# A selective-scan block with a binary MLP: padded loads of u and B, and another order of VectorE's scan step

## What is computed

```python
xc = silu(conv(normed @ in_proj_W[:, :E]) + conv_b)
dt = clip(softplus(xc @ dt_W + dt_b), 0.001, 0.1)      # (8, 512, E)
Bp, Cp = xc @ B_W, xc @ C_W                            # (8, 512, N)
def step(h, ins):                                      # h: (8, E, N)
    x_t, dt_t, B_t, C_t = ins
    dA = exp(dt_t[..., None] * A)
    h = dA * h + dt_t[..., None] * B_t[:, None, :] * x_t[..., None]
    return h, einsum('ben,bn->be', h, C_t)
_, y = scan(step, h0, (xc, dt, Bp, Cp))                # 512 steps in time
y = y * silu(z);  x = x + y @ out_proj_W;  x = x + ffn(rmsnorm(x))
```

## Time and profile before

| what | value |
|---|---|
| median of 3 runs | 1122.29 us (1107.89 to 1122.53) |
| profiled execution, own time | 1115.98 us |
| its span, first to last instruction | 1114.2 us |
| granted TensorE clock, mean | 0.960 |
| PE busy | 967.9 us (87%) |
| DVE busy | 935.2 us (84%) |
| ACT busy | 908.7 us (82%) |
| POOL busy | 847.9 us (76%) |
| DMA moved | 327.39 MB, mean 294 GB/s |

### The profile page before, as it was taken

One profiled execution on the slowest core, in us unless ns is written; L12 is line 12 of the kernel. 1 busy time (PEld: TensorE's weight loads), 2 busy tenths in 40 slices (PEclk: granted clock), 3 DMA queues, 4 the chain that ended last, 5 costly groups with the idle time before them and its releaser, 6 DMA issues.

```text
span 1114.2 us, 27718 instructions
## 1 busy us (share of the span) xinstructions
PE 967.9 (87%) x8006; PEld 426.6 (38%) x8006; DVE 935.2 (84%) x2131; ACT 908.7 (82%) x1093; POOL 847.9 (76%) x1216
## 2 busy tenths in 40 slices
PE   5998883668999999998999887899998899999897
PEld 3555540113333343433333332334343334343436
DVE  5677663799989999997998887899998899999983
ACT  1666776789999999997988887899997899998980
POOL 6555513789888889887888786898887788988880
PEclk9999996789999999999999999899999899999999
DMA  4234358999999999997999999799999799999940
GB/s 139 81 136 180 136 200 298 345 327 355 351 343 334 345 355 350 345 344 268 356 341 332 319 328 318 271 351 352 353 349 333 280 366 343 339 356 340 335 148 10
DMA packets 76758, 327.39 MB, mean 294 GB/s; under 512 B 13472, under 2 KB 32800, under 8 KB 41504
## 3 DMA queue, kind: packets, MB, share of 16 engines
q1 hardware_dynamic: 76576, 325.30, 83.6%
HBM read 303.24 MB, written 22.02 MB: 292 GB/s over the span
## 4 chain that ended last, share of the span: by engine, by line
DVE 27%; PE 25%; POOL 19%; issue 16%; DMA 5%; ACT 5%; SPq 2%; DVEq 1%; POOLq 0%; ACTq 0%
POOL decayed L593 13%; DVE ps L1221 9%; PE ps L798 8%; DVE state L1232 7%; PE ps L743 5%; PE ps L897 5%; DMA decay<-dt_stage 4%; PE ps L883 3%; DVE h L1336 2%; ACT state L1030 2%; DVE h L1345 1%; DVE soft L1147 1%; POOL soft L543 1%; SPq L392 1%; POOL u_rest L553 1%
## 5 line engine op out<-in xcount | busy, mean ns | idle before, releaser
L593 POOL TENSOR_TENSOR decayed<-decay,state 128x256 f32<-128x256 f32 x1024 | 725.5, 733 | 169.1 <-DVE state L1232 125.4
L1010 ACT ACTIVATE decay<-decay,a_col 128x2048 f32<-128x2048 f32 x256 | 512.7, 2003 | 46.3 <-DMA decay<-dt_stage 36.5
L1232 DVE TENSOR_TENSOR state<-decayed,ps 128x256 f32<-128x256 f32 x1024 | 403.1, 417 | 55.4 <-POOL decayed L593 40.0
L1221 DVE TENSOR_TENSOR ps<-decay,ps 128x512 f32<-128x512 f32 x512 | 352.6, 689 | 40.5 <-ACT state L1030 17.2
L1030 ACT COPY state<-ps 128x512 f32<-128x512 f32 x512 | 288.9, 582 | 64.6 <-issue 43.2
L798 PE MATMUL ps<-state,c_cols 128*32 128x256 f32 x4096 | 338.2, 403 | 0.1
L743 PE MATMUL ps<-moving,b_rows 64*128 64x256 bf16 x1024 | 204.3, 281 | 100.5 <-DVE ps L1221 96.3
L750 PE MATMUL ps<-moving,b_rows 64*128 64x256 bf16 x1024 | 205.4, 282 | 12.0 <-DMA b_rows<-b_stage 12.0
L883 PE MATMUL ps<-h,w 128*128 128x256 f32 x512 | 175.8, 429 | 1.0 <-DVE h L1336 0.8
L743 PEld LDWEIGHTS ps<-moving,b_rows 64*128 64x128 bf16 x1024 | 58.4, 94 | 274.0 <-DVE ps L1221 172.3
L798 PEld LDWEIGHTS ps<-state,c_cols 128*32 128x32 f32 x4096 | 82.0, 109 | 113.4 <-issue 101.3
(11 more groups left out here) (124 smaller groups left out, 825.3 us busy)
## 6 DMA issues: line engine op xcount, KB each, us to landing
decay<-dt_stage SPq DMA_DIRECT2D x512, 512.0 KB, 6.6
moving<-u_stage SPq DMA_DIRECT2D x64, 288.0 KB
b_stage<-b_parts SPq DMA_DIRECT2D x24, 384.0 KB, 3.8
b_rows<-b_stage SPq DMA_DIRECT2D x64, 144.0 KB
dt_stage<-dt_tok SPq DMA_DIRECT2D x8, 512.0 KB, 3.1
u_stage<-u_parts SPq DMA_DIRECT2D x8, 512.0 KB, 2.8
x_tok<-in_L_attn_x_dram SPq DMA_DIRECT2D x4, 512.0 KB, 3.5
u_stage<-u_parts SPq DMA_DIRECT2D x8, 256.0 KB, 2.1
```

The costliest lines, as they stand in the source:

```text
L593: nc.gpsimd.tensor_tensor(decayed[:, p], decay[:, dec_slot(m, k), p, k % TS, :], state[:, (k - 1) % RING, p * E:(p + 1) * E], ALU.mult).th ...
L1010: nc.scalar.activation(pair, pair, ACT.Exp, scale=a_col[:, 2:3]).then_inc(decay_ready, 1)
L1221: nc.vector.tensor_tensor(ps[:, acc_bank(m, k), :].rearrange("p (q e) -> p q e", q=HQ), decay[:, dec_slot(m, k), HQ:Q, k % TS, :], ps[:, a ...
L1232: nc.vector.tensor_tensor(state[:, k % RING, p * E:(p + 1) * E], decayed[:, p], ps[:, SELFP + k % 2, p * E:(p + 1) * E], ALU.add).then_inc ...
```

## The change

Two things. First, u_stage and b_stage get a fourth part, NS = NP + 1, that holds zeros. A load of u now reads 16 rows and writes each four times, to 64 partitions, every second one; a load of B reads and writes 64 rows. So all 128 rows of `moving` are written by loads, and the two memsets of `moving` go; those of `b_rows` stay. The zeros are stored once to DRAM in the prologue, by three DMAs for each batch (`store_pads`), from a part of `moving` that POOL fills with zeros. Second, DVE's step does the first self pair's sum ahead of the product in PSUM and the second behind it, then y's copy. PE's, ACT's and POOL's programs of the scan stay as they are.

```diff
-    ROWS = NP * NP * HALF
-    RSTEP = 3
-    RFIRST = HROW + RSTEP - 1 - RSTEP * (ROWS // 2)
+    NS = NP + 1
+    ROWS = NS * NS * HALF
+    assert HQ * ROWS == P
-    u_stage = nc.dram_tensor("u_stage", (HQ, HQ, 2, NP, T, E), BF16, kind="Internal").ap()
+    u_stage = nc.dram_tensor("u_stage", (HQ, HQ, 2, NS, T, E), BF16, kind="Internal").ap()
-    b_stage = nc.dram_tensor("b_stage", (HQ, HQ, 2, NP, NP, T, 2 * N), BF16, kind="Internal").ap()
+    b_stage = nc.dram_tensor("b_stage", (HQ, HQ, 2, NS, NS, T, 2 * N), BF16, kind="Internal").ap()
         def product_rows(hq):
-            first = RFIRST - 2 + hq
-            return slice(first, first + RSTEP * (ROWS - 1) + 1, RSTEP)
+            return slice(hq, P, HQ)
...
-                         .unsqueeze(1).broadcast_to([HALF * NP, NP, TC * E])
+                         .unsqueeze(1).broadcast_to([HALF * NS, NS, TC * E])
...
+                def store_pads(n):
+                    q, bb = n // 2, n % 2
+                    u_rows, b_planes = u_stage[q % HQ, q // HQ, bb], b_stage[q % HQ, q // HQ, bb]
+                    zeros = moving[:, 1, 0:2 * NS].rearrange("p t e -> p (t e)")
+                    sp.dma_start(u_rows[NP].rearrange("(p j) e -> p (j e)", j=NJ),
+                                 zeros[:, 0:NJ * E]).then_inc(pads_stored, 16)
+                    sp.dma_start(b_planes[NP].rearrange("k (p j) n -> p k (j n)", j=NJ),
+                                 zeros[:, 0:NS * NJ * 2 * N].rearrange("p (k n) -> p k n", k=NS)).then_inc(pads_stored, 16)
+                    sp.dma_start(b_planes[0:NP, NP].rearrange("k (p j) n -> p k (j n)", j=NJ),
+                                 zeros[:, 0:NP * NJ * 2 * N].rearrange("p (k n) -> p k n", k=NP)).then_inc(pads_stored, 16)
...
+                sp.wait_ge(pad_zeroed, 1)
+                for n in range(B):
+                    store_pads(n)
                 for q in range(Q):
...
                 sp.wait_ge(rows_zeroed, 2)
+                sp.wait_ge(pads_stored, 16 * PADS)
...
+                nc.gpsimd.memset(moving[:, 1, 0:2 * NS], 0.0).then_inc(pad_zeroed, 1)
...
-                    nc.gpsimd.memset(moving[:, 0], 0.0)
...
-                    nc.vector.memset(moving[:, 1], 0.0)
...
+                    def add_self(p):
+                        wait_step(dve, self_decayed[p], t)
+                        nc.vector.tensor_tensor(state[:, k % RING, p * E:(p + 1) * E], decayed[:, p],
+                                                ps[:, SELFP + k % 2, p * E:(p + 1) * E], ALU.add
+                                                ).then_inc(self_state[p], 1)
+                    wait_step(dve, self_input, t)
+                    wait_step(dve, contracted, t - RING)
+                    add_self(0)
                     dve.wait_ge(acc_state, t + 1)
                     wait_step(dve, acc_copied, t - NACC)
                     nc.vector.tensor_tensor(ps[:, acc_bank(m, k), :].rearrange("p (q e) -> p q e", q=HQ),
...
                                             ).then_inc(acc_decayed, 1)
+                    add_self(1)
                     chunk = i * 2 + k // TC
                     if k % TC == LAG and not (known(t) and t < TC):
                         keep_y(chunk - 1, i + k // TC - 1, (k // TC + 1) % 2)
-                    wait_step(dve, self_input, t)
-                    wait_step(dve, contracted, t - RING)
-                    for p in range(Q // 2):
-                        wait_step(dve, self_decayed[p], t)
-                        nc.vector.tensor_tensor(state[:, k % RING, p * E:(p + 1) * E], decayed[:, p],
...
```

More of the change, by code:

```diff
@@ L46, in mamba_and_binary_mlp_block @@
     HROW = P // 2
-    ROWS = NP * NP * HALF
-    RSTEP = 3
-    RFIRST = HROW + RSTEP - 1 - RSTEP * (ROWS // 2)
-    assert RFIRST > 0 and HROW + HQ - 1 + RSTEP * (ROWS // 2) <= P
+    NS = NP + 1
+    ROWS = NS * NS * HALF
+    assert HQ * ROWS == P
     QE = Q * E
@@ L118, in mamba_and_binary_mlp_block @@
         b_loaded = [sem("b_loaded0"), sem("b_loaded1")]
+        pad_zeroed = sem("pad_zeroed")
         rows_zeroed = sem("rows_zeroed")
+        pads_stored = sem("pads_stored")
         const_set = sem("const_set")
@@ L212, in mamba_and_binary_mlp_block @@
         STORES = 2 + NP
+        PADS = 3 * B
         def batches(eng, slot, filling=None):
@@ L1227, in step @@
                         keep_y(chunk - 1, i + k // TC - 1, (k // TC + 1) % 2)
-                    wait_step(dve, self_input, t)
-                    wait_step(dve, contracted, t - RING)
-                    for p in range(Q // 2):
-                        wait_step(dve, self_decayed[p], t)
-                        nc.vector.tensor_tensor(state[:, k % RING, p * E:(p + 1) * E], decayed[:, p],
-                                                ps[:, SELFP + k % 2, p * E:(p + 1) * E], ALU.add
-                                                ).then_inc(self_state[p], 1)
                     if known(i) and i == 0:
```

## The result

The changed kernel takes 1406.06 us (median of 4 runs, 1401.68 to 1407.72), the kernel before 1122.41 us beside it (4 runs, 1107.89 to 1129.42). The ratio is 1.2575, with a 95% interval of 1.2452 to 1.2698: slower, as forecast, by 284 us where 239 were forecast. The time lies in the range of 1295 to 1435, 51 us above the forecast of 1355. The profiled execution spans 1403.1 us.

A forecast was written before the change was run, and what follows sets the result against it. DVE's own instructions set a 1.65 us step; the new order makes it 2.16. Scan 1037 + 81 + 10 + 20 = 1148 against 909, +239 on the profiled 1115.98, loads and pads zero: 1355 us, range 1295 to 1435.

The forecast's parts named there:

- The ring: In each scan step, DVE's product, PE's input products, contraction, DVE's first sum, next product: 2.16 us against 1.65.
- y's copy: DVE's copy, now behind the second sum, delays the contraction opening each 16-step chunk: 0.33 us in 31 chunks, 10 us.
- The loads and the pads under cover: Larger scan loads (57 to 62 us per 32 steps of 69) and the prologue's stores of zeros stay hidden: nothing.
- The clock in the first steps: First 32 scan steps, little finishing work on PE, clock partly low: 2.6 us a step, between 2.16 and 2.91.
- The later steps: The other 480 scan steps, with PE 71% busy and at full clock: 2.16 us each, 1037 us.
- the 20 us of waits that were kept: In the scan, 6.5 us for the first loads and 13.6 us of DVE's product behind ACT's exponential stay.
- The front: Before the scan, first loads add 2 us, dropped memsets save; together zero (-2 to +2).
- (a): Rival: TensorE at half clock for much of the scan, 2.91 us a step: 1724 us, half of them about 1540; chance 0.08.
- (b): Rival: in the scan the loads bind at 352 GB/s, not DVE's new order: +39, 1155 us; chance 0.05.
- (c): Rival: faster, as POOL starts its first pair sooner and DVE idles less in the scan: at most 61 us, 1055; chance 0.04.
- (d): Rival: both effects, of order and loads, stay under 1% each: 1105 to 1140 us; chance 0.03.

The follow-up runs named there:

- e_order: The kernel before with nothing but the new order of DVE's step, loads of 36 rows: 1402.1 us, ratio 1.2521.
- e_lag2_after: The changed kernel with LAG = 2 instead of 3, so PE issues the contraction one step earlier: 1182.2 us, ratio 1.0522.
- e_half_after: The changed kernel with the contraction over half of its columns in 14 of 16 steps: 1334.9 us, ratio 1.1962.
- e_half_before: The kernel before with the contraction over half of its columns in 14 of 16 steps: 1115.6 us, ratio 0.9996.
- e_warm: The changed kernel with one extra matmul of unused result per step in the first 32 steps: 1390.2 us, ratio 1.2393.
- e_loads: The changed kernel with the old order of DVE's step, keeping the 64-row loads and the zeros: 1180.1 us, ratio 1.056.
- e_pefirst: The changed kernel with PE's contraction ahead of the input products instead of behind them: 1181.6 us, ratio 1.0594.
- e_lag2_order: The kernel before with the new order of DVE's step and LAG = 2, loads of 36 rows: 1127.5 us, ratio 1.0077.

## Why the prediction was right, and which term was too small

**The ring** was the right mechanism and, at full clock with PE's finishing work behind it, the right size. Forecast 2.16 us from five differences of the trace before; measured 2.17 as the median, with each of the five parts as read. In steps with little finishing work it is 2.26 and 2.37, of which the forecast had nothing. e_order shows that the order alone does it, e_lag2_after that without the contraction in it the loss of 224 us is gone, e_half_after that the contraction's length goes into the step one for one, and e_half_before that it did not before.

**y's copy**: forecast +0.33 in 31 steps, measured 2.54 against 2.17, +0.37.

**The loads and the pads under cover**: forecast nothing. e_order and the changed kernel differ by 4 us in 1400, and P's first start is at 183.3 and 183.2 us in them. SP's 24 issues of zeros were slower than a row of before let expect (0.4 to 0.8 us each at first, about 1.2 from then on, but for one of 2.5), and the third x_tok load was issued at 39.41 us instead of 18.52; DVE's statistics that read it still began at 57.52 (57.83 before). DMA's share fell to 0.88 at 282 GB/s; below 0.95 at about 290 was forecast.

**The clock in the first steps**: here lies the step that was too small. The prediction said "I take 2.6 a step" for the first 32 steps and "full clock" for the others. Measured were 2.87 a step in the first 32 (91.8 us; 31 at 2.6, one at 2.16 and a copy make 83.1: +8.7), and 86.9 us in the second 32, where 69.8 follow from the forecast's terms: +17.1. The reasoning failed in three places. A value about midway between 2.16 and 2.91 stands for a clock that is at each level half of the time; but it stayed at the lower one for 143 us on end, and from the fourth step on the first body's step was 2.98 on average. The ring leaves PE idle, and with one more matmul in each step (e_warm) the clock rose. Second, I took the second body for one like the later ones by a mean over 60 us (56.0 us busy), though its first six steps have hardly any finishing work. Third, a busy share was no guide to the level. The earlier trace rows has a clock of 1.00 in both of its stretches, at 45% as at 66%; the low values lie around the first. And in the changed kernel PE was busy 65% from 250 to 310 us at 0.50. It is busy for longer with the same work there, so a share read at one level can't be held against the other. The Trainium skill (TensorE: Matmul & The Clock Gate, Part 1) says that the default is throttled and activity releases it; the stretches of e_warm agree, with 0.50 at 27.07 of 50 us busy and 1.00 at 34.21.

**The later steps**: bodies 2 to 15 took 1011.4 us; 447 x 2.16, 28 copies and the 20 us of waits that were kept make 994.8: +16.6. The waits came to less than the 20: three steps at the ends of a loop round (4.5, 4.4 and 5.8 us) hold 8.2 us over the ring, where the trace of before had 12.4 of its 13.6 us at ACT's exponential, and the 6.5 lay at the front. The 25 steps that a lapse of the clock touches hold 13.3 over 2.16, y's copies 1.3 more than forecast, and all others 13.9, of which about 4 are the difference of 2.17 and 2.16, and others the steps of 2.37 in bodies 2 and 15.

**The front**: P's first start moved from 175.0 to 183.2 us, +8.2. P now stands behind the first sum and so behind the first loads; before, it ran first and its second start waited. I had left that wait (6.5 us) in the scan's sum and so booked it there.

Together 8.7 + 17.1 + 16.6 + 8.2 = 50.6 us, against 50 between the forecast's span and the measured one.

The number came out 4% low and in range. In the third part the waits, 12 us under the forecast, offset about as much as the lapses cost; that is luck.

**The rivals.** (a), half clock for much of the scan: it came for 198 of 1190 us, and its price (2.91 a step) was close, with 2.92 and 3.03 measured. (b), the loads bind: not in this kernel, but e_loads is its case, and there its mechanism was right and its price low. It gave 1155; e_loads took 1180.1. The rate was the mis-sized term: I took 352 GB/s, the best stretch, for 14 of 16 bodies, where 331 is what a body got (336 in e_pefirst, 60.1 us). The estimate worked out from the Trainium skill (DMA: Bandwidth & Descriptors, Why a DMA increments its semaphore by 16 and not by 1) was 1130, by its rule for the number of engines: 12 for 36 rows and 16 for 64. The measurement shows no such gain: 331 to 336 GB/s with the 64 rows and 333 with the 36. (c), faster: e_lag2_order tried it with the ring cut, and it came out 0.8% slower. (d) didn't happen.

## What to carry to other kernels

A wait that is long done where it stands can close a ring when its instruction is moved ahead of the one that the awaited engine itself waits for: list, for each moved wait, which instruction of the other engine satisfies it, what stands ahead of that one in its program, and whether that waits for what you have just put behind. The length of the ring can be added up from the trace of before, link by link, and it came out within 0.01 us of the median step here, but 0.1 to 0.2 short where the awaited engine had little else to do. The cheap cure is to let the other engine's work be issued one step earlier (LAG = 2), not to shorten it; it takes the loss away, but made the new order no faster than the old one.

Costs that hide under one another don't add: the loads' 59 us vanish under the ring's 281, and 55 us of them come back once the ring is cut (1182.2 against 1127.5). And a ring that idles TensorE should be priced at the lower clock wherever the engine has little other work, in every such stretch, not at a mean of the two.

## What the runs showed of the hardware beyond what was expected

TensorE's granted clock sat at its lower level (1.2 GHz) for 143.4 us on end. From 200 to 250 us the engine was busy 27.07 of 50 us there; it was at its upper level (2.4 GHz) in the same steps with one more matmul each, 34.21 of 50. The same contraction took 0.64 us at the one and 1.08 at the other, so the ring was 2.17 us at the one (2.26 and 2.37 in steps with little finishing work) and 2.92 to 3.03 at the other. In the run with half the contraction the mean clock was lower (0.866 against 0.923), and a quarter of the gain was missing.

Sixteen DMA engines gave 331 to 336 GB/s over whole bodies, whether u and B were loaded as 36 rows or as 64; stretches of 60 us with a share of 0.97 or more lay between 314 (e_lag2_after, 850 to 910) and 357 (the kernel before, 370 to 430).
